# The bf16 products that shift the transposed scores, over all 128 rows or as 32-row tiles

## The reference

```python
scores = jnp.einsum('bhqd,bhkd->bhqk', q, k) / np.float32(np.sqrt(HD))
attn = jax.nn.softmax(scores, axis=-1)
out = jnp.einsum('bhqk,bhkd->bhqd', attn, v)
```

## Time and profile before

| | |
|---|---|
| median of 3 runs | 6144.0 us |
| profiled execution | 6155.05 us |
| its span | 6153.3 us |
| TensorE busy | 5445.3 us, 88% |
| VectorE busy | 4576.2 us, 74% |
| ScalarE busy | 3707.2 us, 60% |
| GpSimd busy | 2164.3 us, 35% |
| mean granted TensorE clock | 0.923 |

### The profile page before, as it was taken

One profiled execution on the slowest core, in us unless ns is written; L12 is line 12 of the kernel. 1 busy time (PEld: TensorE's weight loads), 2 busy tenths in 40 slices (PEclk: granted clock), 3 DMA queues, 4 the chain that ended last, 5 costly groups with the idle time before them and its releaser, 6 DMA issues. The chain is left out here.

```text
span 6153.3 us, 112087 instructions
## 1 busy us (share of the span) xinstructions
PE 5445.3 (88%) x39324; PEld 3838.9 (62%) x39324; DVE 4576.2 (74%) x16189; ACT 3707.2 (60%) x9249; POOL 2164.3 (35%) x3076
## 2 busy tenths in 40 slices
PE   7899899888898989898888898989889898898987
PEld 4666566666666666566666666666666666666654
DVE  2477787677887777787777887777887787887784
ACT  3466566665676656666665666656666565666642
POOL 0233433333343333343333443333433233433331
PEclk7799999999999999999999999999999999998976
DMA  2000000000000000000000000000000000000000
GB/s 86 4 6 5 8 8 6 7 8 7 6 6 10 5 7 6 8 8 6 7 8 7 6 6 10 5 7 6 6 10 6 7 5 10 6 6 6 5 4 6
DMA packets 29383, 53.47 MB, mean 9 GB/s; under 512 B 8145, under 2 KB 9810, under 8 KB 27986
## 3 DMA queue, kind: packets, MB, share of 16 engines
q1 hardware_dynamic: 28770, 45.73, 2.4%
HBM read 37.33 MB, written 8.39 MB: 7 GB/s over the span
## 5 line engine op out<-in xcount | busy, mean ns | idle before, releaser
L1032 DVE MATCH_REPLACE8 wk<-m,wk 128x256 f32<-128x256 f32 x2048 | 823.4, 410 | 0.0
L1053 POOL TENSOR_SCALAR mx<-m 128x2 f32<-128x2 f32 x512 | 121.6, 238 | 1918.0 <-DVE wk L1032 1917.9
L1028 DVE MAX8 m<-wk 128x8 f32<-128x256 f32 x2048 | 760.7, 414 | 0.0
L467 DVE TENSOR_REDUCE m_nm<-bankM 128x2 f32<-128x512 f32 x1024 | 652.5, 684 | 126.2 <-PE bankM L457 124.8
L798 ACT ACTIVATE xk_area<-bankH,xb 64x256 f32<-64x256 f32 x1024 | 480.4, 469 | 397.4 <-PE bankH L700 380.1
L1062 POOL TENSOR_TENSOR t_pr<-t_pr,sc 128x512 f32<-128x512 f32 x512 | 651.9, 1273 | 40.2
L1060 POOL TENSOR_TENSOR t_pr<-wk,sc 128x512 f32<-128x512 f32 x512 | 658.9, 1287 | 2.1 <-PE bankT L558 0.9
L989 ACT ACTIVATE t_pr<-t_pr,t_nm 128x256 f32<-128x256 f32 x1024 | 465.0, 507 | 192.0 <-POOL t_pr L1062 191.5
L516 PE MATMUL bankM<-m_q,m_kT 32*128 32x512 f32 x2048 | 572.8, 639 | 0.0
L457 PE MATMUL bankM<-m_kT,m_q 32*128 32x256 f32 x4096 | 546.2, 400 | 8.1 <-DVE m_nm L467 5.7
L558 PE MATMUL bankT<-ident,t_pr 128*128 128x128 f32 x2048 | 350.2, 297 | 115.7 <-ACT t_pr L989 112.9
(11 more groups left out here) (223 smaller groups left out, 11916.4 us busy)
## 6 DMA issues: line engine op xcount, KB each, us to landing
xin<-x_in SPq DMA_DIRECT2D x32, 256.0 KB, 2.6
ctxA<-ctx_in SPq DMA_DIRECT2D x32, 256.0 KB, 2.6
ctxB<-ctx_in SPq DMA_DIRECT2D x32, 256.0 KB, 3.0
out<-x SPq DMA_DIRECT2D x32, 256.0 KB, 2.0
w<-w_w SPq DMA_DIRECT2D x2, 1024.0 KB
xwq<-w_xwq SPq DMA_DIRECT2D x1, 1024.0 KB
xwk<-w_xwk SPq DMA_DIRECT2D x1, 1024.0 KB
xwv<-w_xwv SPq DMA_DIRECT2D x1, 1024.0 KB
```

Of the source, the lines that this page charges most:

```text
L467: nc.vector.tensor_reduce(b["nm"][:, i % 2, 2 * (i // 2) + x, :], banks[u % 4][:].rearrange("p (j s) -> p j s", j=2), AX.X, ALU.max, negat ...
L1028: link.inc(nc.vector.max(top, src[:, t, :]))
L1032: m = nc.vector.match_replace(out=wk[:, k, t, :], in_to_replace=take, in_values=src[:, t, :], imm_value=-BIG)
```

## The change

The bf16 product of line 513 contracts over all 128 rows of `sel_b` and `m3` in place of the 32 rows of the pair's own strip. So that the sum stays the same, the table `sel` is 1 in rows 3k to 3k + 2 of the first strip alone, and zero in the other three.

```diff
@@ at_scores_T
             for x in range(2):
                 r = strip(2 * m + x)[1]
-                nc.tensor.matmul(bank[x][:], sel_b[r:r + 32, 2 * m + x, :], b["m3"][r:r + 32, :], start=True, stop=False, skip_group_check=True)
+                nc.tensor.matmul(bank[x][:], sel_b[:, 2 * m + x, :], b["m3"][:], start=True, stop=False, skip_group_check=True)
@@ layouts
-        "sel": np.broadcast_to((p[:, None] % 32 // 3 == np.arange(QUADS)[None, :])[:, :, None], (P, QUADS, P)), "keyid": tok,
+        "sel": np.broadcast_to((p[:, None] // 3 == np.arange(QUADS)[None, :])[:, :, None], (P, QUADS, P)), "keyid": tok,
```

## The result

Over 20 timed runs each, the changed kernel takes 6166.4 us (median; 6142.3 to 6186.89), the kernel before 6151.86 (6123.77 to 6163.21). The ratio is 1.0027, 95% interval 1.0015 to 1.0039: slower by some 17 us, where +70 was forecast. It is a real difference, but it lies inside the 0.5% that the prediction called no change. The profiled execution took 6160.35 us (6225 forecast). All times and ratios here are of fast executions; the one slow one, 13363.91 us at a granted clock of 0.40 in `delay_thin_mla`, is left out of them.

What follows compares the result with a forecast made beforehand. TensorE bounds most of a lap, VectorE the part before TensorE's two waits per period. 216 - 86 - 50 - 10 = +70 us: 6225 for the profiled execution, 6214 against the median; range 6115 to 6330.

Steps and rivals of the forecast that it cites:

- The stream: TensorE's instruction stream: 0.38 us more per step, 0.42 with half-clock steps counted, over 512 steps: +216 us.
- the second product: In each step, line 513's two products follow one another instead of running side by side: +0.216 us.
- the shape: Change of tile shape between lines 513 and 516 in each step: +0.09 us.
- the open load: First fp32 weights of line 516 loaded in the open after the tile shape switch: +0.11 us, lower bound 0.
- What is hidden: Half the steps, ahead of TensorE's waits before line 756: 80% of their 108 us disappears, -86 us.
- There I let all pass: The other 16 steps of a period, where TensorE is the fuller engine: all 108 us reach the end time.
- The clock: Shorter waits before line 756 remove 60% of the falls to 1.2 GHz, -50 us; the last batch gives -10.
- The price of a fall: Stretch at 1.2 GHz behind TensorE's wait before line 756: 2.6 us lost in the end time.
- A: TensorE bounds throughout; the whole stream cost arrives and the clock gives nothing: 6360 us; chance 0.15.
- B: No measurable change: line 516's weight load hides, waits hide half, clock returns 60: +17, 6161 us; chance 0.19.
- C: All 32 falls behind waits go, clock rises in other thin stretches too: -55, 6089 us; chance 0.14.
- D: The change does not do what it says, as line 513's 32-row pairs did not overlap before; chance 0.02.

Runs made afterwards that it cites:

- delay_thin_mla: Kernel before, with the first 32-row product of each step issued three times in the first attention alone; ratio 0.9955 to the kernel before.
- wide_crs: Kernel before, with the whole-array product of line 513 only in the cross attention; ratio 1.0039 to the kernel before.
- fill_wait: Kernel before, with 16 unread fp32 products of 128 columns in front of TensorE's wait of line 756; ratio 0.9895 to the kernel before.
- delay_thin_more: Kernel before, with the first 32-row product of each step issued five times; ratio 1.0479 to the kernel before.
- wide_twice: Changed kernel, with each whole-array product issued twice; ratio 1.0095 to the kernel before.

## Why the prediction was off

*The stream.* Right: 0.216 for the second product (pair to 516 now 0.53), 0.09 for the shape, 0.11 for the open load (1.06 for 0.95), this also under 512-column records, where I had allowed for 0. The sum at full clock, 195 us, came out as 186. The spacing of 131 ns that the Trainium skill gives (TensorE: Matmul & The Clock Gate, "Back-to-back issue gap") doesn't show here either: the pair of 513 lasts 0.21 us longer than one product of it.

*What is hidden.* The step that failed first, and the largest miss. I hid 86 us in the two waits before 756 and let the 16 steps of the cross attention pass in full, 108 us. TensorE's free time shrank by 119, of which the wait before 756 gave 56 (135 to 79) and the wait of 558 for ScalarE 33. The wait before 756 shrank by 2.0 us a lap and not by the 3.2 that eight steps bring, so 80% there was too much; but the other steps passed far less than in full: wide_crs costs 24 us, not 108. "There I let all pass" was the wrong choice: other waits take delay too (31 us less free time in wide_crs), and the clock pays for more.

*The clock.* The second failed step, and its near hit in size is luck. I had it give 60 us back, 50 of them behind the waits before 756, where 60% of the falls were to go, and 10 in the last batch. But 22 of the loop's 26 laps still have the slow clock there, and the loss around 756 fell by 13 us, in the last 70 us of the kernel by 3. The other 45 or so of the 61 came back in places that I had not named. The price of a fall was right: with the wait filled, fill_wait gets all 68 us around 756 back. What was wrong is that the clock would mostly stay up behind waits shortened to the 3.2 and 2.35 us that came of it, and that it would stay as it was elsewhere. It also rises in wide_crs, whose wait before 756 is untouched (lost 315 for 390 in one execution; mean clock of all 0.934 for 0.922). And it rises there in delay_thin_mla, which leaves the steps of the cross attention alone, so fuller rows are not needed for it. A window over the cross attention's steps of one period, before and after, has the clock 0.80 and 0.93:

```profile
2860.00:2886.00 26.00, 23.34 (x168) 13.65 (x170) 18.86 (x75) 17.50 (x56) 12.59 (x17) 0.80 0.01 2
```

```profile
2858.40:2884.40 26.00, 23.46 (x191) 12.89 (x191) 19.96 (x78) 18.25 (x58) 12.60 (x17) 0.93 0.01 2
```

By the terms, with the 21 us for steps at half clock taken from the stream to the clock: 195 - 86 - 39 = 70 was forecast; 186 - 119 - 61 = 6 is the profiled execution's (5 by the spans). So the stream was 9 us less, the free time took 33 more and the clock gave 22 more, and the median came out 17 above instead of 70. The small result is the difference of large terms that nearly cancel.

*Rivals.* A is out (the wait shrank and the clock rose). B's number, +17, was the measured one, though by another way: its cheaper stream isn't there. C was nearest in kind: it had the clock return something in stretches away from the waits. But its larger term, all 32 falls behind the waits, isn't there either (13 us of 83), and it called a clock over 0.94 the point from which the kernel gets faster; it reached 0.939, with a time just above that of before. D is out.

**Open.** Why the two halves don't add (-34 and +24 against +17) isn't settled; the gap is in the clock, and no run separates the falls of one place from those of another. Nor is it shown why the clock comes back among the steps of the cross attention when only the first attention is delayed. How much fuller rows give at the single dose is not told from the noise; at the double dose the two kernels lie 236 us apart.

## What to carry to other kernels

Price a change on the fullest engine in three terms: its stream, the waits that absorb it, and the clock that filled waits give back; here 186 us of work cost 17. The third can come back far from the wait that was filled, so it is measured and not counted up. Before a slower instruction is accepted for such a gain, fill the wait itself: 8 or 16 unread products in front of it gave 0.6% and 1.05% with the step untouched. Tiles of few rows that run side by side are the cheaper step, but a stretch of mostly such products may run at the slow clock although TensorE is never free, as it did in 8 of the loop's 26 laps in delay_thin_more.

## What the runs showed of the hardware that was not expected

- TensorE without a gap for 27.3 us at 1.2 GHz, in a stretch mostly of 32-row products (8 of the loop's 26 laps of delay_thin_more; the other 18 ran these steps at 2.4 GHz), and at 2.4 GHz in the same steps of every lap with whole-array products (wide_twice): 236 us of 6450 between the two kernels. The Trainium skill (TensorE: Matmul & The Clock Gate, "HAM oscillation — how this bites in real kernels") puts such falls down to idle gaps; this stretch had no gap.
- Delay without use made the kernel faster: 0.427 us more in each of 256 steps, 0.9955 (0.9938 to 0.9972). Most of the clock that it gave back lay among steps that it did not change (141 us lost there before, 97 after).
- Behind waits of equal length (2.35 us) the clock fell in some periods and not in others.
